# Layer norm steps of the attention layers, one turn later in every engine's order

## The reference

```python
h = tok(x)                                   # 16 x 36 tokens, 192 features
h = h + attn(layernorm(h))                   # layer 0: 12 heads of 64, output bias
# layer 1 and the experts (ffn):
x = h + attention(layernorm(h) * g1 + b1)    # layer 1: 12 heads of 16
x = x + moe(layernorm(x) * g2 + b2)          # 8 experts, the best 2 of each token
```

## Time and profile before

| | before |
|---|---|
| median of 3 runs | 435.1 us (432.44 to 436.94) |
| profiled execution | 436.19 us, of which the span of the core's instructions is 434.4 us |
| PE, DVE, ACT, POOL busy | 405.0, 307.9, 239.3, 120.2 us |
| mean granted clock of PE | 0.973 of full speed |
| layer 0's turns from 12 on | 186.7 to 232.1 us of the span |
| layer 1's turns from 12 on | 253.2 to 295.3 us of the span |

### The profile page before, as it was taken

One profiled execution on the slowest core, in us unless ns is written; L12 is line 12 of the kernel. 1 busy time (PEld: TensorE's weight loads), 2 busy tenths in 40 slices (PEclk: granted clock), 3 DMA queues, 4 the chain that ended last, 5 costly groups with the idle time before them and its releaser, 6 DMA issues. The chain is left out here.

```text
span 434.4 us, 8873 instructions
## 1 busy us (share of the span) xinstructions
PE 405.0 (93%) x3079; PEld 331.3 (76%) x3079; DVE 307.9 (71%) x632; ACT 239.3 (55%) x623; POOL 120.2 (28%) x146
## 2 busy tenths in 40 slices
PE   8999899999987899988899988889999999999996
PEld 4336566666687788877677766658999999999986
DVE  1677999999826834578843579745889779789753
ACT  3576888888504157755635766705816526526510
POOL 1202323333104332356622448422122022022000
PEclk9999899999998999999999999859899999999999
DMA  8176443534045021000003000003322232231001
GB/s 170 33 212 124 103 115 101 128 103 120 13 126 216 1 85 56 1 2 2 2 2 127 2 2 3 2 2 127 128 74 71 76 110 62 78 113 54 0 2 41
DMA packets 12444, 30.27 MB, mean 70 GB/s; under 512 B 3949, under 2 KB 6669, under 8 KB 12281
## 3 DMA queue, kind: packets, MB, share of 16 engines
q1 hardware_dynamic: 12168, 29.77, 23.8%
q10 hardware_dynamic: 240, 0.04, 0.1%
HBM read 28.40 MB, written 0.52 MB: 67 GB/s over the span
## 5 line engine op out<-in xcount | busy, mean ns | idle before, releaser
L537 PE MATMUL ps<-weights,hT 120*96 120x288 f32 x320 | 81.6, 411 | 0.0
L537 PEld LDWEIGHTS ps<-weights,hT 120*96 120x96 f32 x320 | 51.7, 166 | 24.0 <-issue 0.8
L1388 PE MATMUL ps<-w,hid_hi 128*128 128x384 f32 (+1 forms) x240 | 67.9, 355 | 1.1 <-DVE rest L1472 1.0
L1415 ACT ACTIVATE hidden<-ps 128x576 f32<-128x576 f32 x48 | 31.1, 648 | 56.9 <-PE ps L1307 54.5
L375 DVE SCALAR_TENSOR_TENSOR weights<-dist_y,hat_x 120x576 f32<-120x576 f32 x80 | 60.4, 795 | 1.8 <-PE ps L537 1.2
L1389 PE MATMUL ps<-w,hid_lo 128*128 128x192 f32 (+1 forms) x240 | 60.1, 250 | 0.0
L1459 DVE TENSOR_TENSOR hid_lo<-hidden,hid_hi 128x576 fp32r<-128x576 f32 x48 | 46.0, 992 | 16.4 <-ACT hid_hi L1419 16.4
L1307 PE MATMUL ps<-x_hi,w_hi 128*128 128x288 f32 x192 | 56.1, 305 | 1.0 <-PEq L949 0.9
L1307 PE MATMUL ps<-x_lo,w_hi 128*128 128x288 f32 x192 | 55.0, 300 | 0.0
L1083 ACT ACTIVATE a_probs<-ps,a_minus_peak 108x108 f32<-108x108 f32 (+1 forms) x144 | 47.2, 341 | 10.8 <-DVE a_minus_peak L1140 10.8
L444 ACT ACTIVATE dist_y<-pos,row_shift 120x576 f32<-120x576 f32 x64 | 46.9, 770 | 2.2 <-DVE weights L375 1.7
(11 more groups left out here) (152 smaller groups left out, 765.5 us busy)
## 6 DMA issues: line engine op xcount, KB each, us to landing
pos<-pos_dram SPq DMA_DIRECT2D x16, 540.0 KB, 4.3
raw<-in_w SPq DMA_DIRECT2D x8, 768.0 KB, 4.2
raw<-in_w SPq DMA_DIRECT2D x8, 576.0 KB, 3.6
patches<-in_patches SPq DMA_DIRECT2D x6, 216.0 KB, 5.7
dcn_w<-in_dcn_w SPq DMA_DIRECT2D x1, 1152.0 KB, 8.7
samples<-extra SPq DMA_DIRECT2D x12, 64.0 KB, 2.1
a_raw<-in_a_wq SPq DMA_DIRECT2D x1, 768.0 KB, 4.8
a_raw<-in_a_wk SPq DMA_DIRECT2D x1, 768.0 KB, 6.0
```

What stands on the lines that cost most here:

```text
L537: ins = nc.tensor.matmul(ps[0:C1, 2 * (b % 2) + a, 0:HALF], hT[:, b % 2, t, :], weights[:, t, a * HALF:(a + 1) * HALF], start=(t == 0), st ...
L1388: nc.tensor.matmul(ps[0:n, 4 + t % 4, 0:2 * DIM], hid_hi[:, s, f, t0:t0 + n], w2[s][:, f, :, :].rearrange("p a d -> p (a d)"), start=(f == ...
L1415: nc.scalar.activation(hidden[:, f % 3, :].rearrange("p (a t) -> p a t", a=2), ps[:, 2 * (f % 2):2 * (f % 2) + 2, 0:HALF], ACT.Gelu).then_ ...
```

## The change

```diff
@@ stage_attention
-        STEP_TURN = (0, 1, 3)
+        STEP_TURN = (1, 2, 4)
         T_TURN = O_TURN + STEP_TURN[1] + 1
         TURNS = O_TURN + UPG * (XT - 1) + STEP_TURN[2] + 1
@@ POOL's list
                     for g in range(XT):
-                        if turn == O_TURN + UPG * g:
+                        if turn == O_TURN + UPG * g + STEP_TURN[0]:
                             for k in range(ROOTS):
                                 inverse_deviation(g, k)
-                        if layer == 1 and turn == O_TURN + UPG * g + 2:
+                        if layer == 1 and turn == O_TURN + UPG * g + STEP_TURN[1] + 1:
                             n = XTILES[g][1]
                             pool.wait_ge(sum_ready, g + 1)
```

## The result

| | before | after |
|---|---|---|
| median, first comparison | 434.37 us (432.44 to 436.94, 4 runs) | 440.22 us (438.37 to 444.39, 4 runs) |
| profiled execution (its span) | 436.19 (434.4) | 444.39 (442.6) |
| layer 0 from turn 12 to the next block | 45.51 us | 54.41 us |
| layer 1's whole block | 63.14 us | 62.73 us |

The ratio is 1.0186 (95% interval 1.013 to 1.0242): slower by 5.9 us at the medians, where 6.0 was forecast. In a second comparison on another occasion it was 439.77 against 433.59, 1.0197 (1.0122 to 1.0272). The profiled execution of after is the slowest of its four, so its 8.2 us are not the effect.

A forecast was written before the change was run, and what follows sets the result against it. PE and DVE hand each other the bound, with 0.1 us of slack in layer 0. Layer 0 4.1, layer 1 0.6 and clock 1.3 sum to 6.0 us, on 435.1 giving 441.1 us; range 434.5 to 445.5.

The forecast's parts named there:

- Step 0 and the slack: Layer 0: sum and statistics delay unit 11's copy less than before, turn 15 0.47 us earlier; DVE's slack is 0.1 us.
- Step 1 and the second root: Layer 0: DVE's later chain, with x waiting for the root, delays turn 16 by 1.4 us (0.9 to 1.6).
- Third period and end of layer 0: Layer 0, turns 20 to the end: turn 24 1.2 us late, +1.3 us for this part together (0.8 to 1.5).
- Layer 1: Layer 1's block: shorter stall before turn 14, later turns and last transposes delayed; +0.6 us in all (-0.6 to 1.5).
- The clock: Layer 0: PE's longer idle times bring one fall to half clock, costing 1.3 us.
- The rule by long gaps: PE's clock falls only by long idle gaps, so gaps of 1.7 us in layer 0 would cost nothing.
- (a): Rival: as forecast, but layer 0's clock does not fall; 439.8 us, chance 0.24.
- (b): Rival: clock falls in both long periods of layer 0, or earlier in layer 1; 442.4 to 444 us, chance 0.18.
- (d): Rival: waits for DVE's copies in both layers vanish without new ones, 5 us faster; 430.1 us, chance 0.10.
- (c): Rival: only the late last transposes cost, 0.9 us in layer 0 and 0.4 in layer 1; 436.4 us, chance 0.12.

The follow-up runs named there:

- Experiment 3: Changed kernel, but sum, statistics and roots stay in the output product's turn in both layers; 435.24 us against before's 433.90, ratio 1.0046.
- Experiment 4: Changed kernel with x and its wait for the second root one turn later in layer 0; 435.94 us against before's 433.77, ratio 1.0052.
- Layer 1 alone: The kernel before with the change made only in layer 1; 435.36 us against before's 433.90, ratio 1.0034.
- after, again: The changed kernel unaltered, measured a second time beside before; 439.77 us against 433.59, ratio 1.0197.
- experiment 5: Changed kernel with 12 filler matmuls on PE behind the transposes of tiles 0 to 2 in layer 0; 438.95 us against before's 433.90, ratio 1.0128.

## Why the prediction was right

The direction, the place and the mechanism in layer 0 held. That the sum came within 0.2 us is luck in part: layer 0 was put about 1.0 too high, and layer 1 too low, by as much as 0.8.

- **Step 0 and the slack.** Predicted: unit 11's copy 3.7 us after turn 13 starts, turn 15 0.47 us early. Measured: 194.34 - 190.65 = 3.69, and 0.48. Experiment 3 shows that in layer 0 step 0's place, and not the rest of the move, makes the cost.
- **Step 1 and the second root.** Predicted 1.4 us for turn 16 (0.9 to 1.6), with a wait of x for the root. Measured 1.28 and 1.24 in the two long periods, with the wait of 0.36 and x at its slow 0.78. The root took 0.57, so the upper end was out. Experiment 4 moved x away and got 1.04 us back.
- **Third period and end of layer 0.** Predicted +1.2 and then +0.1. Measured at full clock, without the 0.51 us of the fillers: +0.91 (turns 20 to 24 10.10 instead of 9.19), and -0.37 from there to the end of the block. The end was made up of -0.6 for `xhat`'s wait and +0.7 for the late last transposes. From turn 24 to the last output product the kernel gained 0.93 (7.34 us instead of 8.27), and from there to the next block it lost 0.57 (7.68 instead of 7.11). Layer 0 in all: 3.1 instead of 4.1, within the bounds of 2.6 to 4.7.
- **Layer 1.** Predicted +0.6 (-0.6 to 1.5). At about the same granted clock (0.94 and 0.95) the block takes 62.00 with the old order and 62.58 to 62.73 with the new one in three profiles: +0.6 to +0.7, with the half clock in other turns. At full clock it comes to more. Layer 1 alone has one stretch of half clock in the block, in turns 16 to 17, which take 6.35 us instead of 5.76; 61.54 - 0.59 is 60.95, against 59.56 for the old order with its fillers: +1.4. That is an estimate from two profiles; the medians of layer 1 alone say +1.5. Turn by turn, turn 16 is 0.47 late, as predicted (0.4), but turn 18 is 1.15 and turn 20 1.75 late (fillers in layer 0, at full clock there), where 0.9 was expected at turn 20. The prediction looked for the delay of turn 18 in POOL's order, with `rest` ahead of the scaling of unit 15. The row names DVE's copy instead, behind the split of the tile, whose first part took 1.79 us beside POOL's weight split instead of 0.48. This term was mis-sized, and the trace shows another wait behind it than the one that was worked out.
- **The clock.** Predicted: one fall in layer 0, 1.3 us. One fall cost 1.34, in one of the three profiles (after, again). The other two have three and four stretches at half clock there, which cost 4.1 and 5.8 us. The median over runs leaves 5.9 - 3.1 = 2.8 us for layer 1 and the clock, so 1.4 to 2.2 for the clock. That is an inference and not a measurement; it fits the 1.3 to 1.8 of experiment 5.
- **The rule by long gaps.** The clock fell behind stalls of at most 1.6 us in all three profiles that have this order of layer 0 without fillers or a moved x. The rule by long gaps (the Trainium skill, TensorE: Matmul & The Clock Gate, HAM oscillation) would have excluded that. The next section of the same page of the Trainium skill, A second HAM failure mode: psum-queue depth-cycling, tells of another kernel in which short idles between groups of matmuls made the clock go up and down. It is the nearer of the two to these traces, whose stalls are of 0.8 to 1.6 us.
- **Rivals.** (a), no fall in layer 0, and (b), several falls, differ from the forecast in the clock alone. No profile of this order shows (a), one shows the forecast and two show (b). The medians of 440.22 and 439.77 lie nearer to (a)'s 439.8 than to the forecast's 441.1 and cannot part them. (d), faster by the removed waits, failed as argued: DVE no longer waits for the output product, but waits longer for the v projection (0.77 instead of 0.30), and step 0 stands behind it. (c) failed on the missing slack.

## What to carry to other kernels

When a step on an in-order engine waits for another engine, look at what the wait hides before moving it: work that starts as soon as its operand is there may lie beside the other engine's long stretch, and the same work a turn later may lie in front of what that engine waits for next. Find for each turn the chain from the last instruction that waits for the other engine to the next one that it waits for, and sum up what stands between; here that sum, with 0.1 us of slack, gave the cost to 0.2 us in each of the two long periods. The sum is only as good as the lengths put into it: an instruction moved beside another engine's work can become several times as long (L115 in layer 1, 1.79 us instead of 0.48), so look at what runs beside its new place as well. An instruction in such a chain whose result nobody needs for a while (x here) is the one to move.

## What was not expected of the hardware

Executions of the same program on one core differ by up to 2%, and the slower ones mostly have the lower granted clock: before ran between 429.5 and 438.4 us on one chip, at 429.5 with a granted clock of 0.992 and at 438.4 with 0.949. One further execution there took 1282.76 us at a granted clock of 1.0, for which nothing here gives a cause. The clock's mean does not set the time alone, since half clock costs little where PE would wait anyway: 3.4 us of it cost 1.34 us in turn 20 of layer 0 and 0.59 in turns 16 to 17 of layer 1. In before, four sets of fillers (2.6 us of matmuls) where PE was about to stall went with full speed through the whole profiled execution, though not through every run, and were worth 1.6 us by the ratio and 3.2 by the medians. Busy time alone does not tell where the clock falls: a stretch with 2.07 us of 3.41 busy (193.76 to 197.17 in after) was followed by full speed, one with 2.35 by half.
